# Zeroing the expert row buffers during the K and V projections instead of during attention

## The reference

```
x = x + tanh(g_xattn) * attention(layernorm(x), ctx)     # 16 heads of 32; q, k, v and the weights
                                                         # are rounded to 8 bits with their own steps
x = x + tanh(g_ffn)   * experts(layernorm(x))            # 16 experts of inner width 352, 4 per token
                                                         # out of 2 of 4 groups; 2 shared experts

q, k, v = xn @ Wq + bq, ctx @ Wk + bk, ctx @ Wv + bv     # q scaled by 1/sqrt(32)
attn    = round8(softmax(q_int @ k_parts))               # unsigned, per row
out     = (attn @ v) @ Wp + bp
h       = silu(x @ W1[e]) * (x @ W3[e]);  y += weight[token, e] * (h @ W2[e])
```

## Time and profile before

| | us |
|---|---|
| median of 3 runs | 1083.51 (1081.62 to 1084.20) |
| profiled execution, its own time | 1084.69 |
| span of its instructions | 1083.1 |
| PE busy | 988.3 (91%) |
| DVE busy | 643.7 (59%) |
| ACT busy | 500.8 (46%) |
| POOL busy | 460.8 (43%) |

### The profile page before, as it was taken

How to read it: one execution, slowest core, us unless ns; L and a number is a source line. 1 busy time by engine, 2 the same in 40 slices (tenths; PEclk the granted TensorE clock), 3 DMA queues, 4 the chain that set the end, 5 groups by cost and what they waited for, 6 DMA issues and landing times.

```text
span 1083.1 us, 16600 instructions
## 1 busy us (share of the span) xinstructions
PE 988.3 (91%) x5718; PEld 499.6 (46%) x5719; DVE 643.7 (59%) x1140; ACT 500.8 (46%) x1072; POOL 460.8 (43%) x352
## 2 busy tenths in 40 slices
PE   5999999879998888998999689999999999999993
PEld 2334444324333333343344356555556556566551
DVE  4895676599998888998899646731111111111146
ACT  2022222369999898998999732111212212212110
POOL 1043333237888787787777700072111111111165
PEclk9999999989999999999999878999999999999996
DMA  9931332588999999999787544053546645643155
GB/s 316 227 97 78 109 105 82 122 169 153 192 189 195 201 194 185 205 203 165 130 136 113 91 168 165 1 204 117 185 155 227 212 173 221 218 170 135 48 159 154
DMA packets 264496, 172.45 MB, mean 159 GB/s; under 512 B 239344, under 2 KB 239344, under 8 KB 262128
## 3 DMA queue, kind: packets, MB, share of 16 engines
q1 hardware_dynamic: 250016, 124.67, 49.3%
q0 software_dynamic: 14416, 46.94, 13.3%
HBM read 68.67 MB, written 44.63 MB: 105 GB/s over the span
## 4 chain that ended last, share of the span: by engine, by line
PE 50%; POOL 21%; DVE 13%; issue 8%; ACT 5%; DMA 2%; SPq 0%; POOLq 0%; DVEq 0%; ACTq 0%
PE ps L685 17%; POOL arena_a L1344 16%; PE ps L705 10%; PE ps L553 6%; PE ps L530 5%; PE ps L570 4%; ACT arena_a L859 3%; DVE span_max L1044 3%; POOL expert_in L1356 2%; PE ps L655 2%; PE ps L612 2%; POOL expert_in L1348 2%; PE ps L715 1%; DVE v_q L1265 1%; PE ps L696 1%
## 5 line engine op out<-in xcount | busy, mean ns | idle before, releaser
L1044 DVE TENSOR_REDUCE span_max<-ps 128x1 f32<-128x481 f32 (+2 forms) x400 | 351.4, 904 | 34.7 <-PE ps L570 28.0
L859 ACT ACTIVATE arena_a<-ps,exp_bias,q_step 128x962 uint8<-128x962 f32 (+1 forms) x288 | 329.9, 1156 | 35.0 <-PE ps L570 15.0
L1344 POOL CAST arena_a<-arena_a 128x3072 bf16<-128x3072 uint8 x100 | 274.3, 2748 | 115.6 <-DMA arena_a<-arena_a 110.2
L570 PE MATMUL ps<-arena_a,q_t 128*128 128x481 bf16 (+1 forms) x864 | 223.1, 372 | 18.6 <-DVE span_max L1044 8.9
L685 PE MATMUL ps<-arena_a,xt 128*128 x544 | 172.3, 459 | 1.7 <-issue 1.7
L1203 DVE TENSOR_TENSOR proj_d<-ps,proj_f 128x352 f32<-128x352 f32 x48 | 25.1, 524 | 205.5 <-ACT proj_f L894 205.4
L705 PE MATMUL ps<-arena_a,proj_r 128*128 (+3 forms) x288 | 134.0, 602 | 0.7 <-ACT proj_r L900 0.7
L900 ACT COPY proj_r<-ps 128x128 f32<-128x128 f32 x144 | 28.4, 270 | 227.1 <-PE ps L696 227.1
L570 PEld LDWEIGHTS ps<-arena_a,q_t 128*128 128x128 bf16 x864 | 62.2, 97 | 147.3 <-ACT arena_a L859 67.2
L685 PEld LDWEIGHTS ps<-arena_a,xt 128*128 128x128 f32 x544 | 100.5, 190 | 61.1 <-issue 17.8
L612 PE MATMUL ps<-v_q,arena_a 128*128 128x32 bf16 (+1 forms) x2400 | 80.2, 180 | 22.7 <-POOL arena_a L1344 20.7
(11 more groups left out here) (168 smaller groups left out, 958.5 us busy)
## 6 DMA issues: line engine op xcount, KB each, us to landing
arena_a<-in_w_up SPq DMA_DIRECT2D x18, 1408.0 KB, 6.4
arena_a<-in_w_down SPq DMA_DIRECT2D x18, 768.0 KB, 8.4
key_parts<-parts SPq DMA_DIRECT2D x23, 512.0 KB, 2.6
expert_in<-proj_r POOLq DMA_DIRECT2D x42, 256.0 KB, 3.6
xt<-expert_in POOLq DMA_DIRECT2D x36, 256.0 KB, 3.0
expert_out<-xt POOLq DMA_DIRECT2D x34, 256.0 KB, 2.3
arena_a<-in_ctx_t SPq DMA_DIRECT2D x3, 1536.0 KB, 13.7
expert_out<-proj_r POOLq DMA_DIRECT2D x17, 256.0 KB, 3.0
```

The costliest lines, as they stand in the source:

```text
L570: last = mm(ps[:, bank + b, 0:w], q_t[:, head, t * P:(t + 1) * P], k_t[head % NK][:, a:a + w], start=True, stop=True)
L859: nc.scalar.activation(halves[:, :, a:a + w], ps[:, bank:bank + 2, 0:w], ACT.Exp, bias=exp_bias[:, n % 2:n % 2 + 1], scale=step_of, accum_ ...
L1044: v.tensor_reduce(span_max[:, n % 2, j:j + 1], ps[:, bank:bank + len(blocks), 0:w], AX.XY, ALU.max).then_inc(s_max, 1)
L1344: p.tensor_copy(p_t[n % NPT].rearrange("p c q -> p (c q)").rearrange("p (j i) -> p j i", j=2), pt_u8[n % NT8].rearrange("p (i j) -> p j i" ...
```

## The change

The 59 stores move. A tile of zeros of 128 by 512 words is now a piece of `xt` beyond the float value row (columns 2944 to 3455); POOL clears it once the seven query tiles have been projected. SP then issues two or three stores of it behind each of the 23 key stores. POOL's memset of `proj_r`, its two waits, and its 59 stores in attention are gone. DVE's memset of the last attention output tile, which overlaps the tile of zeros, now waits until all 59 stores have landed.

```diff
+        zero_tile = xt[:, KPAD:KPAD + D]
...
@@ sync, in the loop over kt, behind the key store
+                if kt == 0:
+                    sp.wait_ge(s_ztile, 1)
+                for rows, a in ZEROED[len(ZEROED) * kt // KT:len(ZEROED) * (kt + 1) // KT]:
+                    sp.dma_start(rows[a * P:(a + 1) * P, :], zero_tile).then_inc(s_xz, 16)
...
@@ vector, between the projections and attention
+            dve.wait_ge(s_xz, 16 * len(ZEROED))
             v.memset(attn[:, T - 1, :], 0.0).then_inc(s_buf, 1)
...
@@ gpsimd, ahead of the loop over kt
+            pool.wait_ge(s_proj, T)
+            p.memset(zero_tile, 0.0).then_inc(s_ztile, 1)
...
@@ gpsimd, behind the loop over kt, and in the attention loop
-            pool.wait_ge(s_mid, KT)
-            pool.wait_ge(s_parts, KT)
-            p.memset(proj_r[:, 0, :], 0.0).then_inc(s_zero, 1)
-            pool.wait_ge(s_zero, 4)
...
-                if 8 <= n < 8 + len(ZEROED):
-                    rows, a = ZEROED[n - 8]
-                    pool.dma_start(rows[a * P:(a + 1) * P, :], proj_r[:, 0, :]).then_inc(s_xz, 16)
```

More of the change, by code:

```diff
@@ L306, in gated_xattn_moe_kernel @@
         s_zero = sem("zeros_ready")
+        s_ztile = sem("zero_tile_ready")
         s_xz = sem("expert_in_zeroed")
```

## The result

The changed kernel takes 1068.57 us (median of 4, 1068.17 to 1069.22) against 1083.86 (median of 4, 1081.62 to 1085.13): a ratio of 0.9861, 95% interval 0.9837 to 0.9885. The forecast was 1071.0, the range 1067.5 to 1077. The profiled execution took 1069.22, its span is 1067.7.

A forecast was written before the change was run, and what follows sets the result against it. In attention's zeroed stretch the landing of transposes on full DMA engines was taken as the bound, elsewhere there ACT, in the projections PE. -13.0 + 0 + 0.5 = -12.5 us on the median 1083.51 gave 1071.0, range 1067.5 to 1077.

The forecast's parts named there:

- Rival A: Attention: zeros were not the cause, the pace with key loads is about 4 anyway; 1084 us, chance 0.05.
- The DMA engines are full there: Attention's stretch with zeros: DMA share 0.99, so the rate at which transposes land sets the end; outside it, ACT does.
- main term: Attention, 66 tiles from tile 9 to tile 75: removing the stores of zeros saves 13.0 us, bounds 9.3 to 15.0.
- upper end: Attention: 66 tiles at 3.70 plus 5.2 us for tail tiles make 249.4 us, a gain of 15.0.
- the tail tiles' price: Attention: tail tiles cost more whatever the DMA does; three at 1.0 us each, plus 2.2 for the aftermath of two.
- aftermath: Attention: the nine tiles behind a tail tile take 1.1 us over the floor; counted twice, 2.2.
- The further 2.0 I held back for late transposes: Attention: gain taken as 13.0 us instead of 15.0, since some transposes would still be late at a share of 0.84.
- The projections: Stage receiving the zeros: PE stays the limit, DMA share rises from 0.31 to about 0.6; counted 0, between 0 and +1.
- The hand-over: Projections to attention: three stores of zeros ahead of head 0's keys cost 0.5 us, between 0 and 1.3.
- B: Attention: the loop of two transposed buffers becomes the bound at 3.90 a tile; 1079 us, chance 0.12.
- D: Projections become DMA-bound, each store of zeros taking 2.5 us instead of 0.72; 1102 us, slower, chance 0.05.

## Why the prediction was right, and where it was off

**What bounds attention.** Right in the outcome, wrong in the reason: the pace falls to ACT's floor once the zeros are out, PE and ACT take POOL's place in the chain, and the whole of it comes out of tiles 9 to 74. Rival A is refuted by the pace of 3.74 with key loads and no zeros, and by 3.72 behind tile 67, where 4.17 had been. "The DMA engines are full there", and the end set by the rate at which transposes land, rested on a share of 0.99; the same bytes on SP behind the transposes ran at 3.81 with a share of 1.05, half of the bytes cost more than half, and small stores ahead of the transposes ran at 3.84 with a share of 0.78. What stands is that the zeros slow the transposes' landing (4.6 against 4.0), that bytes do it (3.73 with POOL's issues and no bytes), and that a third buffer hardly helps against it.

What the pace follows is a delay: the time from the end of a tile's last exponential to the end of its widening. PE's program takes tile n-4's product with the values ahead of the last scores of tile n-1, and ACT waits for those. In the changed kernel PE came to a product that lay ready no sooner than 7.9 us after the tile's last exponential, so a longer delay holds PE up, and ACT behind it. The table gives the means over tiles 9 to 66, worked out from the starts, ends and landings in the traces; the delay is the three parts and the widening of 2.75.

| kernel | exponential to SP's issue | issue to landing | landing to widening | delay | pace |
|---|---|---|---|---|---|
| changed | 0.28 | 4.22 | 0.09 | 7.3 | 3.74 |
| small stores by POOL | 0.30 | 4.20 | 0.20 | 7.5 | 3.73 |
| zeros by SP, behind the transpose | 0.97 | 4.16 | 0.08 | 8.0 | 3.81 |
| small stores ahead of the transpose | 1.36 | 3.99 | 0.06 | 8.2 | 3.84 |
| half of the zeros | 0.79 | 4.57 | 0.22 | 8.3 | 3.88 |
| before, third buffer | 0.25 | 5.12 | 0.30 | 8.4 | 3.93 |
| before | 1.13 | 4.83 | 0.15 | 8.9 | 3.98 |
| zeros by SP, ahead of the transpose | 1.79 | 4.42 | 0.08 | 9.0 | 4.07 |
| zeros by POOL, ahead of the widening | 1.34 | 4.47 | 1.03 | 9.6 | 4.24 |

From 8.0 us up delay and pace rise together whichever part has grown, and whether the DMA share is 0.78 or 1.05; at 7.5 and below the pace stays at 3.73 to 3.75, in the profiles that are not in the table too. In the kernel before PE started 37 of these 58 products within 0.1 us of the end of their widening, in the changed kernel 10. That much the traces show. Why the same bytes lengthen the landing on POOL's queue (4.83) and not on SP's behind the transpose (4.16) is open; moving POOL's stores to another moment did not settle it.

**The size of the main term.** 13.0 forecast, 17.8 measured, over my upper end of 15.0. The term that was mis-sized is the tail tiles' price, 1.0 us of tile 74's own and 1.1 of aftermath. Now the tile behind tile 74 begins 3.68 after it, and so it does in all the other profiles but that of the kernel before, even where zeros run up to tile 66. So its own surcharge is 0: the 4.68 in the earlier trace rows was one late tile of one execution, in which PE waited 0.83 us for POOL's widening, read as the tile's nature. The nine tiles behind it stay dear, 34.93 - 9 x 3.70 = 1.6 over the floor in the changed kernel where 1.1 had been. Without the 3.0 the upper end's formula reads 66 x 3.70 + 2.2 = 246.4 against 246.5 measured; with 1.6 for each aftermath it would be 247.4, so some of that agreement is luck. The further 2.0 I held back for late transposes did not come either.

**The projections.** Counted as 0; the key stores span 141.5 us instead of 141.2, from 61.8 to 203.2. The share is 0.58 where I said about 0.6. SP's issue is 0.63 and not 0.33, which its slack hid. The price of 0.72 a store, taken from output stores, nearly held: from 62 to 200 SP's queue went from 29.5% to 56.6%, which is 0.67 for each of 56 stores.

**The hand-over.** +0.5 forecast, nothing measured. By the ring order that the Trainium skill states (DMA: Bandwidth & Descriptors, section Queues, rings and completion order) it would have been 1.3; the keys did not make PE wait at all. In attention, where a transpose is waited for, the order on SP does cost: 4.07 against 3.81, with a mean landing of 4.42 against 4.16. There the trace agrees with the order; at the hand-over the slack hid it.

**The rivals.** B's mechanism, the loop of buffers, was not at work in the changed kernel, where a third buffer gained nothing; in the kernel before it had a small part, 3.98 to 3.93. D did not come near. The -12.5 forecast became -15.3; the sum was kept low by the tail tiles (3.0), the held-back 2.0 and the hand-over (0.5), and the profiled execution gave back 1.7 ahead of tile 9, nearly all of it to the clock, and 0.7 behind tile 75. That the time still fell in the range is in part luck: the gain of the main term lies outside its own bounds of 9.3 to 15.0, and 1.6 us less, with the full clock that the profile of the kernel before had at the hand-over, the median of 1068.57 would have been 1067.0, under the range's lower end of 1067.5.

## What to carry to other kernels

Ask of a slow stage how long a tile takes from one engine to the next, and how long the order of the waiting engine allows; the busy share of the DMA engines did not tell which kernel was slow. Take bulk stores without a deadline out of a stage whose pace hangs on the landing of transfers, and put them where an engine other than DMA is full and the short transfers have slack; a stage that merely looks quiet can have a 16 KB move on its path. If they must stay, issue them on the same queue directly behind the transfer that is waited for: here 0.17 us a tile against POOL's queue, and 0.25 against the place ahead of the transpose, some 14 us over the stage. And do not read a surcharge off a single tile of a single execution.

## What the hardware showed that was not expected

- Packet times can add up to more than the engines: 104.6% for one queue over 221 us, at a faster pace than with 98%.
- The same 256 KB stores cost 0.08, 0.24 or 0.33 us a tile by queue and place.
- PE's clock was at 1.2 GHz for a stretch of value products behind 3.41 us of idleness in the changed kernel and in four kernels without zeros there, and at 2.4 GHz behind the same idleness in the profiled kernel before and in that with a third buffer: 1.6 us that need no zeros.
